# Down products of the scan stage summed over eight blocks instead of four, with two gate/up weight buffers

## The chip, the cores and the metric

The kernel runs on one core of one Trainium2 chip. The metric is the device time of one execution in microseconds, as the median of several runs. The engines are called PE (matrix products), DVE (vector), ACT (activation), POOL (GpSimd) and SP (which issues nearly all transfers of this stage, in one queue, in program order).

## The reference

Two layers work on x (4 x 512 tokens, 512 wide). Layer 0 is a cross attention and a feed-forward part; layer 1 a selective scan (an SSM whose input is the context and whose gate is x) and a mixture of 16 experts. The stage that matters here computes two parts at once: the feed-forward part of layer 0

```python
x = fwht(x * SU_ug) / SCALE
x_up = x @ W_up.T * (Wscale_ug[:INTER] * SCALE)
x_gate = x @ W_gate.T * (Wscale_ug[INTER:] * SCALE)
x = jax.nn.silu(x_gate) * x_up                        # 2048 wide
x = fwht(x * SU_dp) / SCALE
x = x @ W_down.T * (Wscale_dp * SCALE)                # back to 512
```

and the scan of layer 1, for 4 batches, 512 channels, 16 states, 512 steps

```python
state = state * exp(d_t * A) + (d_t * u_t) * B_t
y_t = einsum('ben,bn->be', state, C_t)
```

followed by `(y + D * u) * silu(z)`, which is added to x.

## The kernel before

`build` runs the stages one after another: norm, attention, prep, mix, norm and router, experts, combine. The change is in `stage_mix` (L1383), the scan stage. It has 64 blocks s, 16 (j) for each of 4 batches (b). A block does the work of one 128-wide slice of the 2048 hidden values and one state n of the scan, for 4 groups t of 128 channels. Each engine has its own program in a fixed order; semaphores are the only tie between them.

- PE, block s (L1623): `gate(s + 2)` and `up(s + 2)`, 12 products each of 512 columns; then `down(s - LAG)`, L1579: CHUNK = 4 fp32 products of 512 columns, which the profile shows as 8 passes, for one of the four groups of 128 tokens. So the downs of 4 blocks lie in the 4 blocks behind them, one token group in each, and each sums over CHUNK blocks in the one bank `ps_y`. Between them lie `turn` (j = 4, 5: transposes of the normed x), `rotate` (j = 7, 8, 10, 11: the Hadamard product of the next batch, 8 fp32 passes) and `turn_gated` (j = 12, 13). `up` has one bank, `ps_u`, and waits for the inner product before it.
- DVE, block s (L1914): `scan(4(s+1))`, `inner(s + 1)` (L1864: silu(gate) x up into `hT`), `add_y` (L1870: the down of the PE block before, from `ps_y` into the residual `xs`), `scan` twice, then what the block has besides (statistics at j = 0 to 3, `spread` at j = 4, low parts of the rotation at j = 8, 9, 11, 12, `add_gated` at 13, 14), and the last `scan`. A scan is the recurrence L1839 and the product with C, L1850; a group t = 0 also has an add, L1856.
- POOL (L1810): the driving products L1786 and the sums over states L1771, 7 operations in a block; at j = 1, 2, 3 `skip_add` (D x u, L1797 and L1799), at 8 to 11 `gated`. ACT: the decays and silu. Both state tiles (2) and drive tiles (4) are rings.
- SP (L1521), block s: `load_gu(s + 3)` (1 MB, waits for up of block s), `load_rows(s + 3)` (2 x 256 KB, waits for the products of block s - 1), at s % 4 == 3 `load_wd` (1 MB), then `load_u` at j = 0, 2, 3, `load_du` at j = 7 to 10 and `load_delta` at j = 11, 12, 14.
- Buffers: `gu` 3 x 1 MB, `wd` 2 x 1 MB, `hT` 2 x 4 slices, `delta` 6, `du` 8.

Of the kernel before, what the change touches and what calls it, by code (L numbers as in the profile page):

```python
# [17 lines left out]
P = 128  # L18
B = 4
S = 512  # L20
# [1362 lines left out]
def stage_mix(nc, xs, uT0, hs, guT, wdT, Wscale_ug, SU_dp, A_log, skip, u_d, delta_d, du_d, bc_d, ident):  # L1383
# [3 lines left out]
    ALL = B * BLOCKS  # L1387
    CHUNK = 4
    UNITS = BLOCKS * ET
    GU, ROWS, RING, BANKS = 3, 3, 4, 2  # L1390
    DELTAS, DUS = 6, 8
    LAG = CHUNK - 1
# [13 lines left out]
    with Scope(nc, "mix") as m:  # L1406
# [17 lines left out]
        gu = [m.sb(f"gu{i}", [P, 2, 2, KD, P], F32R) for i in range(GU)]  # L1424
        wd = [m.sb(f"wd{i}", [P, CHUNK, DIM]) for i in range(2)]
        sil = [m.sb(f"sil{i}", [P, S]) for i in range(2)]
        hT = [m.sb(f"hT{i}", [P, CHUNK, S]) for i in range(2)]
        delta = [m.sb(f"delta{i}", [P, S]) for i in range(DELTAS)]
# [13 lines left out]
        s_gu = [m.sem(f"gu_in{i}") for i in range(GU)]  # L1442
        s_wd = [m.sem(f"wd_in{i}") for i in range(2)]
        s_rows = [m.sem(f"rows_in{i}") for i in range(ROWS)]
# [13 lines left out]
        with m.block() as block:  # L1458
            @block.sync
            def _(sp):  # L1460
# [5 lines left out]
                def load_wd(n):  # L1466
                    if n >= 2:
                        sp.wait_ge(s_y, TB * (n - 1))
                    sp.dma_start(wd[n % 2][:, :, :], wdT[:, n % CHUNK * CHUNK:(n % CHUNK + 1) * CHUNK, :]).then_inc(s_wd[n % 2], 16)

# [44 lines left out]
                load_rows(1)  # L1515
                load_gu(2)
                load_rows(2)
                load_wd(0)
                load_wd(1)

                for s in range(ALL):  # L1521
                    b, j = divmod(s, BLOCKS)
                    if 3 <= s + 3 < ALL:
                        load_gu(s + 3)
                    if s + 3 < ALL:
                        load_rows(s + 3)
                    if s % CHUNK == CHUNK - 1 and 2 <= (s + 1) // CHUNK < ALL // CHUNK:
                        load_wd((s + 1) // CHUNK)
                    if b >= 1 and j == 0:
                        load_u(b - 1, 0)  # L1530
                        load_u(b - 1, 1)
                    if b >= 1 and j == 2:
                        load_u(b - 1, 2)
                    if b >= 1 and j == 3:
                        load_u(b - 1, 3)
                    if b + 1 < B and 7 <= j < 11:
                        load_du(ET * (b + 1) + j - 7)
                    if b + 1 < B and j in (11, 12):
                        load_delta(ET * (b + 1) + j - 11)
                    if b + 1 < B and j == BLOCKS - 2:  # L1540
                        load_delta(ET * (b + 1) + 2)
                        load_delta(ET * (b + 1) + 3)
# [4 lines left out]
            def _(pe):  # L1547
# [22 lines left out]
                def down(n):  # L1570
                    c, t = divmod(n, TB)
                    if t == 0:
                        pe.wait_ge(s_h, CHUNK * (c + 1))
                        pe.wait_ge(s_wd[c % 2], 16 * (c // 2 + 1))
                    if n:
                        pe.wait_ge(s_yadd, n)
                    tok = slice(t * P, (t + 1) * P)
                    for k in range(CHUNK):
                        mm = pe.matmul(ps_y[:, :], hT[c % 2][:, k, tok], wd[c % 2][:, k, :], start=(k == 0), stop=(k == CHUNK - 1))  # L1579
                    mm.then_inc(s_y, 1)  # L1580
# [42 lines left out]
                for s in range(ALL):  # L1623
                    b, j = divmod(s, BLOCKS)
                    if s + 2 < ALL:
                        gate(s + 2)
                        up(s + 2)
                    if s >= LAG:
                        down(s - LAG)
                    if b + 1 < B:  # L1630
# [14 lines left out]
                    if b >= 1:  # L1645
# [3 lines left out]
                        if j == 13:  # L1649
                            turn_gated(b - 1, 2)  # L1650
                            turn_gated(b - 1, 3)
                for n in range(ALL - LAG, ALL):
                    down(n)
# [176 lines left out]
            def _(dve):  # L1830
# [27 lines left out]
                def inner(n):  # L1858
                    j = n % BLOCKS
                    dve.wait_ge(s_up, n + 1)  # L1860
                    dve.wait_ge(s_silu, n + 1)
                    if n >= 2 * CHUNK and n % CHUNK == 0:
                        dve.wait_ge(s_y, TB * (n // CHUNK - 1))
                    dve.scalar_tensor_tensor(hT[n // CHUNK % 2][:, n % CHUNK, :], ps_u[:, :], upsc[:, j:j + 1],  # L1864
                                             sil[n % 2][:, :], ALU.mult, ALU.mult).then_inc(s_h, 1)

                def add_y(n):
                    dve.wait_ge(s_y, n + 1)
                    row = xs[:, n // BLOCKS * TB + n % TB, :]
                    dve.tensor_tensor(row, ps_y[:, :], row, ALU.add).then_inc(s_yadd, 1)  # L1870
# [4 lines left out]
                def gate_stats(b, t):  # L1875
                    dve.wait_ge(s_yadd, BLOCKS * b + (CHUNK - 1) * TB + t + 1)
                    own.mark(dve.bn_stats(stats[:, TB + t, :], xs[:, b * TB + t, :]))
# [36 lines left out]
                for s in range(ALL):  # L1914
                    b, j = divmod(s, BLOCKS)
                    q = ET * (s + 1)
                    if s + 1 < ALL:
                        scan(q)
                        inner(s + 1)
                    if s > LAG:  # L1920
                        add_y(s - LAG - 1)
                    if s + 1 < ALL:
# [29 lines left out]
                    if s + 1 < ALL:  # L1952
                        scan(q + 3)
                for n in range(ALL - LAG - 1, ALL):
                    add_y(n)
# [816 lines left out]
```

## Time and profile before

| | |
|---|---|
| median of 3 runs | 2685.6 us (2676.52 to 2686.33) |
| profiled execution | 2678.03 us, of which the span is 2676.2 us |
| mean granted clock of PE | 0.926 of full speed |
| scan stage | 1434 to 2175 us of the span |
| busy in the stage: PE, DVE, POOL, ACT | 660.2, 666.9, 606.5, 418.4 us of 741 |
| PE clock, transfers in the stage | 0.95; 171 GB/s |

The profile is one execution. A line of the timeline gives start, duration, engine, source line, the operation, what it writes and reads; a bracket at the end says how long the engine was idle before it and who ended that. A line of L1579 with x8 is eight passes, merged. Busy time isn't pace: the distance between two starts of the same operation (L1864 here, once in a block) is.

### The profile page before, as it was taken

The numbers are of one execution on the slowest core, as the hardware profiler recorded it, in microseconds if no ns is written. First come the engines' busy times: TensorE is split into PE (matmuls) and PEld (weight loads), VectorE is DVE, ScalarE is ACT, GpSimd is POOL, SyncE is SP. The second block draws the span as 40 slices with busy tenths as digits, with TensorE's granted clock in tenths as the row PEclk, the third lists the DMA queues.
The fourth block names the chain that finished last, engine by engine and source line by source line (L and its number), as shares of the span: only waits on it lengthen the run. The fifth ranks groups of instructions, "written<-read, shape, count | busy, mean of one in ns | idle before, by whom it ended". The sixth has DMA issues, their size and how long they took to land. (4 is left out here: it accounts for less than half of the span.)

```text
span 2676.2 us, 35075 instructions
## 1 busy us (share of the span) xinstructions
PE 2285.0 (85%) x10784; PEld 1760.5 (66%) x10785; DVE 1848.7 (69%) x3381; ACT 1229.4 (46%) x2129; POOL 1354.8 (51%) x1088
## 2 busy tenths in 40 slices
PE   3799999999999999998774998897998969468980
PEld 2688888878888888887433665665665547347770
DVE  6577776767676777766775999999999976312223
ACT  2344444544454544444573655655655622124430
POOL 0233333333333333333584888878978931678324
PEclk7799999999999999999887999998998988789995
DMA  7512232222323122220557555564665321765317
GB/s 283 221 67 88 87 111 88 85 74 84 111 87 112 68 87 87 87 88 20 185 194 226 173 183 189 172 197 142 208 183 163 122 83 48 248 170 176 121 51 263
DMA packets 136761, 363.49 MB, mean 136 GB/s; under 512 B 21264, under 2 KB 58768, under 8 KB 118416
## 3 DMA queue, kind: packets, MB, share of 16 engines
q1 hardware_dynamic: 123504, 328.30, 35.8%
q0 software_dynamic: 6320, 20.71, 2.5%
q10 hardware_dynamic: 6768, 12.32, 1.2%
q8 instruction: 94, 1.54, 0.2%
q14 instruction: 75, 0.61, 0.1%
HBM read 289.99 MB, written 71.30 MB: 135 GB/s over the span
## 5 line engine op out<-in xcount | busy, mean ns | idle before, releaser
L641 POOL TENSOR_SCALAR att_probs<-att_probs,att_recip 128x512 f32<-128x512 f32 x256 | 182.1, 714 | 560.8 <-DVE att_recip L708 560.8
L1786 POOL TENSOR_TENSOR mix_drive<-mix_du,mix_rows 128x512 f32<-128x512 f32 x256 | 326.7, 1283 | 63.0 <-DMA mix_rows<-bc_d 24.5
L565 ACT ACTIVATE att_probs<-att_s,att_bias,att_rq 128x512 f32<-128x512 f32 x256 | 200.5, 783 | 287.6 <-DVE att_bias L704 287.2
L1839 DVE TENSOR_TENSOR_SCAN mix_state<-mix_state,mix_drive 128x512 f32<-128x512 f32 x256 | 312.7, 1221 | 16.1 <-POOL mix_drive L1786 11.6
L1670 ACT ACTIVATE mix_state<-mix_delta,mix_a 128x512 f32<-128x512 f32 x256 | 176.7, 691 | 278.4 <-DVE mix_drive L1850 238.6
L1771 POOL TENSOR_TENSOR mix_y<-mix_y,mix_drive 128x512 f32<-128x512 f32 x180 | 230.8, 1282 | 78.7 <-DVE mix_drive L1850 78.7
L1579 PE MATMUL mix_down<-mix_wd,mix_hT 128*128 128x512 f32 x512 | 232.7, 597 | 8.6 <-DVE residual_x L1870 8.6
L703 DVE TENSOR_REDUCE att_nmax<-att_s 128x1 f32<-128x512 f32 x256 | 174.9, 683 | 69.3 <-PE att_s L101 62.0
L744 DVE TENSOR_TENSOR att_pT<-att_pt,att_pT 128x512 fp32r<-128x512 f32 x256 | 170.0, 685 | 65.6 <-ACT att_pT L571 61.6
L571 ACT CAST att_pT<-att_pt 128x512 fp32r<-128x512 f32 x256 | 144.2, 593 | 133.0 <-PE att_pt L422 128.7
L99 PE MATMUL att_w<-att_w_qkv,att_cx 128*128 128x256 f32 x512 | 158.4, 309 | 34.5 <-DVE att_w_qkv L690 26.4
L1579 PEld LDWEIGHTS mix_down<-mix_wd,mix_hT 128*128 128x128 f32 x512 | 97.5, 191 | 110.5 <-issue 96.2
L101 PE MATMUL att_w<-att_w_qkv,att_cx 128*128 128x256 f32 x512 | 152.5, 298 | 0.0
L100 PE MATMUL att_w<-att_w_qkv,att_cx 128*128 128x256 f32 x512 | 152.3, 297 | 0.0
L422 PE MATMUL att_pt<-att_ident,att_probs 128*128 128x128 f32 x1024 | 142.1, 277 | 6.6 <-DVE att_pT L744 2.3
L650 POOL TENSOR_TENSOR att_rq<-att_qss,att_power 128x8 f32<-128x8 f32 x32 | 55.6, 1737 | 159.2 <-DVE att_qss L740 159.2
L422 PEld LDWEIGHTS att_pt<-att_ident,att_probs 128*128 128x128 f32 x1024 | 118.8, 144 | 22.1 <-DVE att_pT L744 12.0
L99 PEld LDWEIGHTS att_w<-att_w_qkv,att_cx 128*128 128x128 f32 x512 | 105.0, 205 | 39.8 <-issue 37.3
L1850 DVE TENSOR_TENSOR mix_drive<-mix_state,mix_rows 128x512 f32<-128x512 f32 x180 | 124.4, 691 | 6.2
L99 PE MATMUL exp_g<-exp_w,exp_xT 128*128 x188 | 81.9, 436 | 53.2 <-POOL exp_w L2525 34.8
L579 ACT CAST att_oT<-att_o 128x512 fp32r<-128x512 f32 x64 | 37.7, 589 | 181.0 <-PE att_o L101 181.0
L99 PE MATMUL att_s<-att_kT,att_qT 128*128 128x512 f32 x256 | 106.7, 417 | 14.0 <-issue 9.1
(356 smaller groups left out, 6655.5 us busy)
## 6 DMA issues: line engine op xcount, KB each, us to landing
att_xn<-normT SPq DMA_DIRECT2D x32, 2048.0 KB, 8.7
mix_gu<-guT SPq DMA_DIRECT2D x64, 1024.0 KB, 8.2
mix_rows<-bc_d SPq DMA_DIRECT2D x128, 256.0 KB, 5.1
guT<-att_ffnT SPq DMA_DIRECT2D x32, 512.0 KB, 5.7
mix_wd<-wdT SPq DMA_DIRECT2D x16, 1024.0 KB, 7.8
slots<-exp_y ACTq DMA_DIRECT2D x47, 256.0 KB, 2.0
normT<-nrm_outT SPq DMA_DIRECT2D x4, 2048.0 KB, 9.1
exp_raw<-in_L_ffn_Wg SPq DMA_DIRECT2D x16, 512.0 KB, 5.8
```

The costliest lines, as they stand in the source:

```text
L99: pe.matmul(out, lh, rh, start=start, stop=False)
L101: return pe.matmul(out, ll, rh, start=False, stop=stop)
L422: tr = pe.transpose(ps_pt[(b + n) % 2][:, t, :], probs[:, h * TB + t, k * P:(k + 1) * P], ident_sb[:, :])
L565: act.activation(probs[:, n, :], ps_s[n % 2][:, :], ACT.Exp, bias=bias[:, n:n + 1], scale=rq[:, n:n + 1], accum_out=sums[:, n:n + 1]).then ...
L641: pool.tensor_scalar(probs[:, n, :], probs[:, n, :], recip[:, n:n + 1], 1.0, ALU.mult, ALU.mult).then_inc(s_pn, 1)
L703: own.after(dve.tensor_reduce(nmax[:, n:n + 1], ps_s[n % 2][:, :], AX_X, ALU.max, negate=True))
L744: dve.tensor_tensor(pT[:, 1, k, :], ps_pt[(b + (TB + 1) * h + k) % 2][:, :, :].rearrange("p t n -> p (t n)"), pT[:, 0, k, :].bitcast(F32), ...
L1579: mm = pe.matmul(ps_y[:, :], hT[c % 2][:, k, tok], wd[c % 2][:, k, :], start=(k == 0), stop=(k == CHUNK - 1))
L1670: act.activation(state[q % BANKS][:, :], delta[i % DELTAS][:, :], ACT.Exp, scale=a[:, t, n:n + 1]).then_inc(s_decay, 1)
L1771: pool.tensor_tensor(out[:, :], out[:, :], drive[q % RING][:, :], ALU.add).then_inc(s_padd, 1)
L1786: pool.tensor_tensor(drive[q % RING][:, :], du[i % DUS][:, :], rows[g % ROWS][:, 0, :], ALU.mult).then_inc(s_drive, 1)
L1839: dve.tensor_tensor_scan(h[:, :], h[:, :], drive[q % RING][:, :], 0.0, ALU.mult, ALU.add).then_inc(s_scan, 1)
```

## The change

Each down now sums over CHUNK = 8 blocks, so there are DOWNS = 32 of them instead of 64, each with 8 products (16 passes). They still take one token group at a time, one in each PE block, in the four blocks s with s - 7 = 0 to 3 modulo 8; the other four blocks have none. The adds follow, one block later. LAG grows from 3 to 7. `hT` becomes a ring of 14 single slices in place of two halves of 4. `wd` holds 8 slices (2 MB) in one buffer, and its load waits until all four downs of the chunk before are made; it is issued at s % 8 == 3 behind `load_rows`. `gu` has two buffers instead of three, and is loaded two blocks ahead; `du` has six instead of eight, and the last two tiles of a batch are loaded at j = 14.

```diff
@@ -1385,10 +1385,12 @@
     INTER = SU_dp.shape[0]
     BLOCKS = INTER // P
     ALL = B * BLOCKS
-    CHUNK = 4
+    CHUNK, INNERS = 8, 14
+    PER = TB * BLOCKS // CHUNK
+    DOWNS = B * PER
     UNITS = BLOCKS * ET
-    GU, ROWS, RING, BANKS = 3, 3, 4, 2
-    DELTAS, DUS = 6, 8
+    GU, ROWS, RING, BANKS = 2, 3, 4, 2
+    DELTAS, DUS = 6, 6
     LAG = CHUNK - 1
     SC = DIM ** -0.5
     assert BLOCKS == STATES
@@ -1422,9 +1424,9 @@
         normT = m.sb("normT", [P, KD, S])
         uT = [uT0, m.sb("uT1", [P, 2, KD, S], F32R)]
         gu = [m.sb(f"gu{i}", [P, 2, 2, KD, P], F32R) for i in range(GU)]
-        wd = [m.sb(f"wd{i}", [P, CHUNK, DIM]) for i in range(2)]
+        wd = m.sb("wd", [P, CHUNK, DIM])
         sil = [m.sb(f"sil{i}", [P, S]) for i in range(2)]
-        hT = [m.sb(f"hT{i}", [P, CHUNK, S]) for i in range(2)]
+        hT = [m.sb(f"hT{i}", [P, S]) for i in range(INNERS)]
         delta = [m.sb(f"delta{i}", [P, S]) for i in range(DELTAS)]
         du = [m.sb(f"du{i}", [P, S]) for i in range(DUS)]
         rows = [m.sb(f"rows{i}", [P, 2, S]) for i in range(ROWS)]
@@ -1440,7 +1442,7 @@
         s_a, s_aexp, s_neg = m.sem("a_in"), m.sem("a_exp_done"), m.sem("a_done")
         s_upsc = m.sem("up_scale_done")
         s_gu = [m.sem(f"gu_in{i}") for i in range(GU)]
-        s_wd = [m.sem(f"wd_in{i}") for i in range(2)]
+        s_wd = m.sem("wd_in")
         s_rows = [m.sem(f"rows_in{i}") for i in range(ROWS)]
         s_delta = [m.sem(f"delta_in{i}") for i in range(DELTAS)]
         s_du = [m.sem(f"du_in{i}") for i in range(DUS)]
@@ -1464,9 +1466,10 @@
                     sp.dma_start(gu[n % GU][:, :, :, :, :].bitcast(F32), guT[n % BLOCKS]).then_inc(s_gu[n % GU], 16)
 
                 def load_wd(n):
-                    if n >= 2:
-                        sp.wait_ge(s_y, TB * (n - 1))
-                    sp.dma_start(wd[n % 2][:, :, :], wdT[:, n % CHUNK * CHUNK:(n % CHUNK + 1) * CHUNK, :]).then_inc(s_wd[n % 2], 16)
+                    if n:
+                        sp.wait_ge(s_y, TB * n)
+                    at = n * CHUNK % BLOCKS
+                    sp.dma_start(wd[:, :, :], wdT[:, at:at + CHUNK, :]).then_inc(s_wd, 16)
 
                 def load_rows(g):
                     b, n = divmod(g, STATES)
@@ -1513,19 +1516,17 @@
                 sp.dma_start(d[:, :], skip.rearrange("(t p) -> p t", p=P), allow_slow_non_contiguous=True).then_inc(s_const, 16)
                 load_gu(1)
                 load_rows(1)
-                load_gu(2)
                 load_rows(2)
                 load_wd(0)
-                load_wd(1)
 
                 for s in range(ALL):
                     b, j = divmod(s, BLOCKS)
-                    if 3 <= s + 3 < ALL:
-                        load_gu(s + 3)
+                    if s + 2 < ALL:
+                        load_gu(s + 2)
                     if s + 3 < ALL:
                         load_rows(s + 3)
-                    if s % CHUNK == CHUNK - 1 and 2 <= (s + 1) // CHUNK < ALL // CHUNK:
-                        load_wd((s + 1) // CHUNK)
+                    if s > CHUNK and s % CHUNK == TB - 1:
+                        load_wd(s // CHUNK)
                     if b >= 1 and j == 0:
                         load_u(b - 1, 0)
                         load_u(b - 1, 1)
@@ -1533,11 +1534,13 @@
                         load_u(b - 1, 2)
                     if b >= 1 and j == 3:
                         load_u(b - 1, 3)
-                    if b + 1 < B and 7 <= j < 11:
+                    if b + 1 < B and j in (7, 8):
                         load_du(ET * (b + 1) + j - 7)
                     if b + 1 < B and j in (11, 12):
                         load_delta(ET * (b + 1) + j - 11)
                     if b + 1 < B and j == BLOCKS - 2:
+                        load_du(ET * (b + 1) + 2)
+                        load_du(ET * (b + 1) + 3)
                         load_delta(ET * (b + 1) + 2)
                         load_delta(ET * (b + 1) + 3)
                 for t in range(ET):
@@ -1571,12 +1574,12 @@
                     c, t = divmod(n, TB)
                     if t == 0:
                         pe.wait_ge(s_h, CHUNK * (c + 1))
-                        pe.wait_ge(s_wd[c % 2], 16 * (c // 2 + 1))
+                        pe.wait_ge(s_wd, 16 * (c + 1))
                     if n:
                         pe.wait_ge(s_yadd, n)
                     tok = slice(t * P, (t + 1) * P)
                     for k in range(CHUNK):
-                        mm = pe.matmul(ps_y[:, :], hT[c % 2][:, k, tok], wd[c % 2][:, k, :], start=(k == 0), stop=(k == CHUNK - 1))
+                        mm = pe.matmul(ps_y[:, :], hT[(c * CHUNK + k) % INNERS][:, tok], wd[:, k, :], start=(k == 0), stop=(k == CHUNK - 1))
                     mm.then_inc(s_y, 1)
 
                 def turn(b, t):
@@ -1625,8 +1628,9 @@
                     if s + 2 < ALL:
                         gate(s + 2)
                         up(s + 2)
-                    if s >= LAG:
-                        down(s - LAG)
+                    c, r = divmod(s - LAG, CHUNK)
+                    if s >= LAG and r < TB:
+                        down(c * TB + r)
                     if b + 1 < B:
                         if j == 4:
                             turn(b + 1, 0)
@@ -1649,7 +1653,7 @@
                         if j == 13:
                             turn_gated(b - 1, 2)
                             turn_gated(b - 1, 3)
-                for n in range(ALL - LAG, ALL):
+                for n in range(DOWNS - TB + 1, DOWNS):
                     down(n)
                 for t in range(TB):
                     turn_gated(B - 1, t)
@@ -1859,21 +1863,21 @@
                     j = n % BLOCKS
                     dve.wait_ge(s_up, n + 1)
                     dve.wait_ge(s_silu, n + 1)
-                    if n >= 2 * CHUNK and n % CHUNK == 0:
-                        dve.wait_ge(s_y, TB * (n // CHUNK - 1))
-                    dve.scalar_tensor_tensor(hT[n // CHUNK % 2][:, n % CHUNK, :], ps_u[:, :], upsc[:, j:j + 1],
+                    if n >= INNERS:
+                        dve.wait_ge(s_y, TB * ((n - INNERS) // CHUNK + 1))
+                    dve.scalar_tensor_tensor(hT[n % INNERS][:, :], ps_u[:, :], upsc[:, j:j + 1],
                                              sil[n % 2][:, :], ALU.mult, ALU.mult).then_inc(s_h, 1)
 
                 def add_y(n):
                     dve.wait_ge(s_y, n + 1)
-                    row = xs[:, n // BLOCKS * TB + n % TB, :]
+                    row = xs[:, n // PER * TB + n % TB, :]
                     dve.tensor_tensor(row, ps_y[:, :], row, ALU.add).then_inc(s_yadd, 1)
 
                 def normal_stats(b, t):
                     own.mark(dve.bn_stats(stats[:, t, :], xs[:, b * TB + t, :]))
 
                 def gate_stats(b, t):
-                    dve.wait_ge(s_yadd, BLOCKS * b + (CHUNK - 1) * TB + t + 1)
+                    dve.wait_ge(s_yadd, PER * (b + 1) - TB + t + 1)
                     own.mark(dve.bn_stats(stats[:, TB + t, :], xs[:, b * TB + t, :]))
 
                 def spread(first, last):
@@ -1917,8 +1921,9 @@
                     if s + 1 < ALL:
                         scan(q)
                         inner(s + 1)
-                    if s > LAG:
-                        add_y(s - LAG - 1)
+                    c, r = divmod(s - LAG - 1, CHUNK)
+                    if s > LAG and r < TB:
+                        add_y(c * TB + r)
                     if s + 1 < ALL:
                         scan(q + 1)
                         scan(q + 2)
@@ -1951,7 +1956,7 @@
                             add_gated(b - 1, 3)
                     if s + 1 < ALL:
                         scan(q + 3)
-                for n in range(ALL - LAG - 1, ALL):
+                for n in range(DOWNS - TB, DOWNS):
                     add_y(n)
                     gate_stats(B - 1, n % TB)
                 dve.wait_ge(s_z, TB * (B - 1))
```

## Rows read from the trace of the kernel before

**Rows 1.** The page, busy time, share of the span and instructions of each engine

```profile
PE 2285.0 (85%) x10784; PEld 1760.5 (66%) x10785; DVE 1848.7 (69%) x3381; ACT 1229.4 (46%) x2129; POOL 1354.8 (51%) x1088
```

**Rows 2.** Groups of the scan stage: count, busy us, mean ns, idle before, releasers

```profile
L1839 DVE TENSOR_TENSOR_SCAN mix_state<-mix_state,mix_drive 128x512 f32<-128x512 f32 x256 | 312.7, 1221 | 16.1 <-POOL mix_drive L1786 11.6 <-ACT mix_state L1670 4.5
L1579 PE MATMUL mix_down<-mix_wd,mix_hT 128*128 128x512 f32 x512 | 232.7, 597 | 8.6 <-DVE residual_x L1870 8.6
L1771 POOL TENSOR_TENSOR mix_y<-mix_y,mix_drive 128x512 f32<-128x512 f32 x180 | 230.8, 1282 | 78.7 <-DVE mix_drive L1850 78.7
```

**Rows 3.** Timeline of DVE, a plain block: start, us, operation, idle before

```profile
1523.96 0.75 DVE L1864 SCALAR_TENSOR_TENSOR mix_hT<-mix_up,mix_up_scale,mix_sil 128x512 f32<-128x512 f32 x1 [0.15 <-ACT mix_sil L1678]
1524.63 0.68 DVE L1870 TENSOR_TENSOR residual_x<-mix_down,residual_x 128x512 f32<-128x512 f32 x1
1525.23 1.22 DVE L1839 TENSOR_TENSOR_SCAN mix_state<-mix_state,mix_drive 128x512 f32<-128x512 f32 x1
...
1533.73 0.75 DVE L1864 SCALAR_TENSOR_TENSOR mix_hT<-mix_up,mix_up_scale,mix_sil 128x512 f32<-128x512 f32 x1 [0.16 <-ACT mix_sil L1678]
```

**Rows 4.** Timeline of PE, a block with a down and a rotation

```profile
1524.77 0.51 PE L99 MATMUL mix_up<-first_uT,mix_gu 128*128 128x512 f32 x1
...
1527.65 3.59 PE L1579 MATMUL mix_down<-mix_wd,mix_hT 128*128 128x512 f32 x8
1531.09 3.60 PE L1601 MATMUL mix_spare<-mix_normT,first_hs 128*128 128x512 f32 x8
1534.12 0.79 PE L99 MATMUL mix_gate<-first_uT,mix_gu 128*128 128x512 f32 x1
...
1537.28 0.39 PE L99 MATMUL mix_up<-first_uT,mix_gu 128*128 128x512 f32 x1
```

**Rows 5.** Adds of DVE that wait for a down: one of them, and all

```profile
1589.72 0.69 DVE L1870 TENSOR_TENSOR residual_x<-mix_down,residual_x 128x512 f32<-128x512 f32 x1 [1.91 <-PE mix_down L1579]
...
  DVE residual_x L1870: 24.9, 13
```

**Rows 6.** PE after blocks without a down, and the clock of that stretch

```profile
1479.71 0.51 PE L99 MATMUL mix_up<-first_uT,mix_gu 128*128 128x512 f32 x1 [2.36 <-DVE mix_hT L1864]
...
1484.16 2.31 PE L1579 MATMUL mix_down<-mix_wd,mix_hT 128*128 128x512 f32 x5
...
1450.00:1484.00 34.00, 25.25 (x88) 19.32 (x87) 32.72 (x40) 20.83 (x25) 28.89 (x23) 0.85 0.57 176
```

**Rows 7.** SP, POOL and DVE around u, block j = 3, batch 1

```profile
1649.79 0.43 SPq L1500 DMA_DIRECT2D mix_work<-u_d  x1
...
1658.76 1.56 POOL L1797 TENSOR_SCALAR mix_work<-mix_work,mix_skip 128x512 f32<-128x512 f32 x1 [1.43 <-DMA mix_work<-u_d]
...
1663.03 1.23 DVE L1839 TENSOR_TENSOR_SCAN mix_state<-mix_state,mix_drive 128x512 f32<-128x512 f32 x1 [2.58 <-POOL mix_drive L1786]
```

**Rows 8.** Transfers: the page's median landing; 1648 to 1661 us in 40 slices

```profile
mix_gu<-guT SPq DMA_DIRECT2D x64, 1024.0 KB, 8.2
...
GB/s 0 0 0 0 63 195 176 164 95 82 113 88 50 101 158 258 315 303 340 347 328 384 391 391 435 447 378 410 454 429 479 391 378 328 202 101 50 25 25 0
...
mix_gu<-guT SPq DMA_DIRECT2D x1, 1024.0 KB, 10.8
```

**Rows 9.** SP and DVE: a load of gu is issued, L1864 follows

```profile
1691.57 0.43 SPq L1464 DMA_DIRECT2D mix_gu<-guT  x1
...
1693.53 0.75 DVE L1864 SCALAR_TENSOR_TENSOR mix_hT<-mix_up,mix_up_scale,mix_sil 128x512 f32<-128x512 f32 x1
```

**Rows 10.** DVE, the last inner product and the last adds

```profile
2134.28 0.75 DVE L1864 SCALAR_TENSOR_TENSOR mix_hT<-mix_up,mix_up_scale,mix_sil 128x512 f32<-128x512 f32 x1 [0.16 <-ACT mix_sil L1678]
...
2146.86 0.69 DVE L1870 TENSOR_TENSOR residual_x<-mix_down,residual_x 128x512 f32<-128x512 f32 x1 [3.85 <-PE mix_down L1579]
...
2151.35 0.69 DVE L1870 TENSOR_TENSOR residual_x<-mix_down,residual_x 128x512 f32<-128x512 f32 x1 [3.06 <-PE mix_down L1579]
...
2160.31 0.69 DVE L1870 TENSOR_TENSOR residual_x<-mix_down,residual_x 128x512 f32<-128x512 f32 x1 [3.06 <-PE mix_down L1579]
```

## Prediction

> **What bounds the kernel now.** I read the page first, for busy shares over the whole span [rows 1], then the groups of the scan stage alone (1434 to 2175 us, 741 us long) [rows 2], then the order of time of single blocks on DVE and on PE [rows 3, 4], and last the lines with an idle time in brackets [rows 5 to 7]. No engine's share of the whole span says anything on a change to one stage; the spacing of blocks does. The reader is to see in [rows 3] that DVE's inner product L1864 comes again after 9.77 us (1523.96 to 1533.73), with only 0.16 us of idle time ahead of it: in a plain block DVE sets the pace. The add L1870 costs it 0.60 us there (1524.63 to the scan at 1525.23).
>
> PE is close behind. From [rows 4]: up starts 0.81 us after L1864 (whose 0.75 us it must await, for `ps_u` has one bank), the down follows up by 2.88 us, eight passes of it take 3.59 us (3.44 us until the next fp32 product can start), gate starts 3.03 us after the last group of eight began, and the next up 3.16 us after gate. A block costs PE 3.03 + 3.16 + about 2.8 = 8.9 us with a down, and 3.44 us more with a rotation, so 12.4 us. Where rotations lie, PE falls back and DVE's adds wait for the down [rows 5]: 1.91 us in that row, 24.9 us in 13 waits in all. Four of these are at the end of the stage (3.85 and three of 3.06 us, together 13.0) [rows 10], so nine inside are worth 11.9 us. That wait decides this change: in program order the add of a down stands right behind the inner product of the next block, so DVE gives a down hardly a block's time.
>
> **The change part by part.** I write b for the batch, j for the block in it, and "burst" for the four blocks in a row that now hold a long down.
>
> (1) Removed: 32 of 64 adds. One, at the stage's end, leaves a wait and not a block; 31 × 0.60 = -18.6 us. POOL is the next engine there: it has 7 products of 1.28 us in a block and only 0.65 to 0.7 us idle in a plain one (78.7 us over the stage [rows 2]), so it nearly fills 9.1 of the new 9.17 us. If it takes half the gain, the term is -9; I take -18.6, as POOL's waits are on DVE.
>
> (2) Moved: the same 512 passes on PE, but 16 in each of four blocks and none in the next four. A long down takes 15 × 0.43 + 0.59 = 7.03 us, from 3.44/8 = 0.43 us a pass [rows 4]. The first add of a burst is wanted 9.17 + 0.67 = 9.84 us after the last L1864; the down ends at 0.81 + 2.88 + 7.03 = 10.72: wait 0.9 us. After that PE's block is 8.9 + 3.44 = 12.35 us without and 15.8 us with a rotation, and each add of a burst waits for what DVE's block lacks of it. DVE's blocks: 9.77 us plain; an estimate from the add's 0.60 us for each further 128x512 operation (statistics, low part of a rotation).
> - Bursts in the middle of batches 0 to 2 (adds at j = 8 to 11; rotations in PE's blocks 7 and 8, so between adds 0, 1 and 2): 0.9 + (15.8 - 10.4) × 2 + (12.3 - 9.8) = 14.2 us each, 42.6 in all.
> - Bursts at the start of batches 1 and 2 (adds at j = 0 to 3, two statistics a block): 0.9 + 3 × (12.35 - 10.95) = 5.1 each; batch 3 (one statistic): 0.9 + 3 × 2.1 = 7.2; together 17.4.
> - The burst in the middle of batch 3, no rotation: 0.9 + 3 × 2.57 = 8.6.
> Sum +68.6 us. The nine waits of 11.9 us that are there now lie in blocks j = 11 to 15, which have no down afterwards: -11.9.
>
> (3) PE's clock. Blocks without a down exist today, at the stage's start: with gaps of 2.4 to 3.9 us the mean granted clock of that stretch is 0.85 and up-to-down takes 1484.16 - 1479.71 = 4.45 us instead of 2.88 [rows 6]: the engine came out of its gap at the lower of its two levels (1.2 GHz). Before each of the seven bursts there are now such blocks (PE has 5.6 us of work in 9.17). Bounds 0 and 1.57 us a burst; I take half, 0.8 × 7 = +5.6, since the late weights (5) will split the gap.
> The Trainium skill speaks against the change here ("TensorE: Matmul & The Clock Gate", the section on why this matters): keep the engine fed, as gaps between bursts of products return it to half its clock. The trace agrees, by [rows 6]. By that rule in full the term is +11.0.
>
> (4) `wd` has one buffer of 2 MB instead of two of 1 MB. Its load waits on SP for the burst's last down (L1467, `s_y`), and what is queued behind it there are, at j = 3, `load_u(b - 1, 3)`, and the next weights. Today u is issued at 1649.79 behind an already free `wd`, and POOL starts with it at 1658.76 after waiting 1.43 us; the chain through POOL reaches DVE's scan at 1663.03, 4.27 us later, which waited 2.58 [rows 7]. Afterwards u is issued when the last down of the burst has ended. It then took 8.9 us to land, with half a megabyte of rows and 1 MB of wd ahead; now 2 MB ahead, at the near 400 GB/s of [rows 8] 2.6 us more, and the rows gone before: 8 us (bounds 7.5 and 11.5). The scan can start 0.8 + 8 + 4.27 = 13.0 us after the down's end. DVE would want it after an add, three scans and the statistics, at 7.5 (batch 3: 6.9): +5.5, +5.5, +6.1 = +17.1. All seven waits of scans for POOL now there, 11.6 us [rows 2], are in blocks 3 to 5 of batches 1 to 3, and the burst's delays give POOL the time: -11.6. The load itself has four blocks (37 us) before the next burst needs it.
> The Trainium skill ("Trainium Kernel Development and Optimization", Best Practices) says to double-buffer so that transfers lie beside compute; by that the single `wd` would stall PE. The trace speaks against a stall of PE, with 8 us of landing against 37, and for one of what is queued behind.
>
> (5) `gu` with two buffers. Each load has the same wait as before (up of block s), and is issued as now, 1.96 us ahead of L1864 [rows 9], but is used one block earlier. It lands 8.2 us after issue, behind a wd after 10.8 [rows 8]: 6.2 us after L1864, where gate could have started at 3.6. Gate then ends at 9.1, before up may start (9.97). Cost 0 to DVE; if the load comes 5 us later in a burst's first block, up to 5 us a burst.
> (6) `du` with six buffers: tiles 2 and 3 are loaded at j = 14, with delta 2 and 3 as now; half a megabyte more, 1.3 us, with their use a block later: 0. `hT` as ring of 14: inner(14) awaits a down that ended two blocks before: 0.
> (7) The stage's end. Today the last add starts 2160.31 - 2134.28 = 26.0 us after the last L1864, in steps of 4.49 us [rows 10]. Afterwards the first long down takes about 8.8 us from a cold engine and starts at 0.9, the other three come in steps of 4.49 + 3.44 = 7.93: 0.9 + 8.8 + 3 × 7.93 = 33.5: +7.5.
>
> Sum: -18.6 + 68.6 - 11.9 + 5.6 + 17.1 - 11.6 + 7.5 = +56.7 us, on the profiled execution's 2678.0: 2734.7. That execution is 7.6 us under the median of three, between the lowest and the others; half of that gives 2738. Bounds: without clock and u terms +45; with the whole clock term, u at its late end and half the saving +80.
>
> **The rivals.**
> - *Faster: PE absorbs the bursts.* The adds are what counts, DVE goes on as the bound, PE runs ahead in the light blocks: -18.6, 2659. It decides at the first add of a burst: the long down must end within 9.84 us of the last L1864, which needs passes of 0.37 us or PE more than a block ahead. Against it: up waits for L1864 in each block, so no lead is kept over light blocks, and [rows 5]. Within it lies "no change", where half is absorbed by slack that I have not seen.
> - *Half of it.* PE's lead at a burst's start is larger than I allow, or u lands in time, or blocks with statistics hide the rest: +25 to +35, about 2708. For it: blocks 4 to 6 are long, and DVE has slack in none but these.
> - *The loads decide.* 2 MB in front of gu at j = 3 and 11, gate misses its weights by 5 us in each of seven bursts: +35 on top, 2770. For it: 10.8 us of landing in [rows 8], above the median; against it: in my sum gate wants them 11 us after their issue.
> - *It doesn't do what it says*: the ring or the one `wd` makes DVE wait in every block. By the counts in (6) it does not.
>
> **How the numbers follow.** My case (+45 to +80, 2723 to 2758) 0.65, half of it 0.13, loads 0.12, no change 0.05, faster 0.05. Within 0.5% (13 us) is what a measurement here can't tell from no change. The range leaves out the two last and some of the loads: 2702 to 2768. Faster 0.05, same 0.05, slower 0.90.
>
> **What would show it.** Right: DVE waits on `mix_down` of some 70 us over four blocks in eight, with 5.4 us at the adds behind rotations; L1870 32 times; the spacing of L1864 at 9.17 us in light blocks, 12.3 in bursts, 15.8 behind rotations; the scan of j = 4 waiting 5 us for POOL, and POOL for u; up from a cold clock at the first block of a burst. Wrong: adds without a wait in a burst (the first rival), or PE's gate waiting for `mix_gu` (the third).

## The result, and the profile after

The changed kernel takes 2749.25 us (median of 4 runs, 2745.28 to 2750.74) against 2681.06 us of the kernel before (4 runs): a ratio of 1.0252, 95% interval 1.0229 to 1.0275. Run again beside another experiment it gave 1.0246 (1.0226 to 1.0265). So it is some 66 to 69 us slower; 57 us had been forecast, and the time lies inside the stated range.

The scan stage, taken from the first inner product to the last add of a down, lasts 779.3 us in the profiled execution instead of 716.1: +63.1. The stages ahead of it, whose code is the same, took 6.3 us longer in that execution. Over the twelve profiled executions of this study, whose kernels are alike up to there but for the stage's own first loads, the first inner product starts anywhere from 1444.2 to 1452.3 us. So I compare stage lengths below wherever a few microseconds count. A stage length is that of one execution; the two of the changed kernel are 2.4 us apart (779.3 and 781.7).

The page, busy time after (the row that answers to [rows 1]), and the groups of the stage that answer to [rows 2]:

```profile
PE 2301.7 (84%) x10784; PEld 1771.6 (65%) x10785; DVE 1835.3 (67%) x3349; ACT 1228.6 (45%) x2129; POOL 1354.3 (49%) x1088
...
L1843 DVE TENSOR_TENSOR_SCAN mix_state<-mix_state,mix_drive 128x512 f32<-128x512 f32 x256 | 312.6, 1221 | 24.3 <-POOL mix_drive L1790 19.0 <-ACT mix_state L1674 5.1
L1775 POOL TENSOR_TENSOR mix_y<-mix_y,mix_drive 128x512 f32<-128x512 f32 x180 | 230.4, 1280 | 113.5 <-DVE mix_drive L1854 112.9
L1582 PE MATMUL mix_down<-mix_wd,mix_hT 128*128 128x512 f32 x512 | 226.8, 596 | 6.3 <-DVE mix_hT L1868 4.0 <-DVE residual_x L1874 2.4
```

DVE has 32 instructions fewer and less work, and yet the kernel is slower. PE still does 512 passes at the same price. What grew is idle time. Here is all of the adds' waiting, from the view of the `mix_down` tile (who waited for it: us, times), in place of the 24.9 us of [rows 5]:

```profile
  DVE residual_x L1874: 94.7, 32
```

A light block and a block of a burst on DVE (timeline; answers to [rows 3]):

```profile
1519.31 0.75 DVE L1868 SCALAR_TENSOR_TENSOR mix_hT<-mix_up,mix_up_scale,mix_sil 128x512 f32<-128x512 f32 x1
1519.98 1.22 DVE L1843 TENSOR_TENSOR_SCAN mix_state<-mix_state,mix_drive 128x512 f32<-128x512 f32 x1
...
1528.49 0.75 DVE L1868 SCALAR_TENSOR_TENSOR mix_hT<-mix_up,mix_up_scale,mix_sil 128x512 f32<-128x512 f32 x1 [0.17 <-ACT mix_sil L1682]
...
1548.92 0.75 DVE L1868 SCALAR_TENSOR_TENSOR mix_hT<-mix_up,mix_up_scale,mix_sil 128x512 f32<-128x512 f32 x1 [0.16 <-ACT mix_sil L1682]
1555.02 0.69 DVE L1874 TENSOR_TENSOR residual_x<-mix_down,residual_x 128x512 f32<-128x512 f32 x1 [5.35 <-PE mix_down L1582]
...
1564.74 0.75 DVE L1868 SCALAR_TENSOR_TENSOR mix_hT<-mix_up,mix_up_scale,mix_sil 128x512 f32<-128x512 f32 x1 [0.17 <-ACT mix_sil L1682]
```

Without its add a block takes 9.18 us, for the 9.17 of the sum; inside a burst, behind a rotation, 15.82 us, of which the add waits 5.35. PE in that burst (answers to [rows 4]):

```profile
1529.29 0.50 PE L99 MATMUL mix_up<-first_uT,mix_gu 128*128 128x512 f32 x1 [1.01 <-DVE mix_hT L1868]
...
1532.15 7.03 PE L1582 MATMUL mix_down<-mix_wd,mix_hT 128*128 128x512 f32 x16
1539.02 3.60 PE L1604 MATMUL mix_spare<-mix_normT,first_hs 128*128 128x512 f32 x8
1542.05 0.79 PE L99 MATMUL mix_gate<-first_uT,mix_gu 128*128 128x512 f32 x1
...
1545.21 0.39 PE L99 MATMUL mix_up<-first_uT,mix_gu 128*128 128x512 f32 x1
```

From up to up PE needs 15.92 us here, with no idle time between; a plain block of a burst is 12.32 us in DVE's spacing. The down is 7.03 us long, and starts 2.86 us after up: PE came into this burst at its full clock.

### The profile page after: what moved, and what is told of

Its sections match the earlier page's. It is cut to its first block and busy times, and to the rows that moved or that the text cites. A ratio compares the mean times of both kernels' runs of the same rounds, so it can differ in the third digit from the quotient of the medians.

```text
span 2743.5 us, 35027 instructions
## 1 busy us (share of the span) xinstructions
PE 2301.7 (84%) x10784; PEld 1771.6 (65%) x10785; DVE 1835.3 (67%) x3349; ACT 1228.6 (45%) x2129; POOL 1354.3 (49%) x1088
## 3 DMA queue, kind: packets, MB, share of 16 engines
q10 hardware_dynamic: 6768, 12.32, 1.2%
## 5 line engine op out<-in xcount | busy, mean ns | idle before, releaser
L1582 PE MATMUL mix_down<-mix_wd,mix_hT 128*128 128x512 f32 x512 | 226.8, 596 | 6.3 <-DVE mix_hT L1868 4.0
L99 PE MATMUL att_w<-att_w_qkv,att_cx 128*128 128x256 f32 x512 | 158.0, 309 | 34.4 <-DVE att_w_qkv L690 26.2
```

The lines of the kernel that those rows point to most:

```text
L99: pe.matmul(out, lh, rh, start=start, stop=False)
L1582: mm = pe.matmul(ps_y[:, :], hT[(c * CHUNK + k) % INNERS][:, tok], wd[:, k, :], start=(k == 0), stop=(k == CHUNK - 1))
```

## The experiments

Ten runs in three groups, beside the two kernels; each run's ratio is to the kernel before on its own chip.

| run | ratio to before (95%) | stage, us | adds' waits before the stage's end | scans for POOL |
|---|---|---|---|---|
| before | 1 | 716.1 | 11.8 | 11.6 |
| after | 1.0252 (1.0229 to 1.0275) | 779.3 | 73.3 | 19.0 |
| after again | 1.0246 (1.0226 to 1.0265) | 781.7 | 75.4 | 19.0 |
| two gu buffers alone | 0.9991 (0.9977 to 1.0005) | 714.4 | 11.2 | 10.3 |
| and six du | 0.9988 (0.9975 to 1.0001) | 715.4 | 12.1 | 10.7 |
| half the products | 0.9920 (0.9901 to 0.9939) | 695.9 | 7.1 | 17.4 |
| u first | 1.0153 (1.0136 to 1.0170) | 760.6 | 75.4 | 0 |
| add late | 1.0239 (1.0213 to 1.0265) | 781.0 | 33.7 | 29.8 |
| gu ahead of du | 1.0229 (1.0205 to 1.0254) | 774.6 | 68.3 | 19.0 |
| three orders | 1.0111 (1.0087 to 1.0134) | 744.8 | 29.2 | 0 |
| spread | 1.0050 (1.0030 to 1.0069) | 726.9 | 12.5 | 0 |
| short rotation | 1.0181 (1.0164 to 1.0198) | 765.2 | 59.5 | 18.8 |

The two last columns are sums of the bracketed idle times of the add and of the scan over the stage's timeline.

### Do the buffers cost anything? (e1, e1b)

```diff
-    GU, ROWS, RING, BANKS = 3, 3, 4, 2
+    GU, ROWS, RING, BANKS = 2, 3, 4, 2
...
-                load_gu(2)
...
-                    if 3 <= s + 3 < ALL:
-                        load_gu(s + 3)
+                    if s + 2 < ALL:
+                        load_gu(s + 2)
```

> The kernel before with two gate/up buffers instead of three (loads two blocks ahead), and nothing else. Theory (long downs on PE are the cost, the buffers are nearly free): gate wants its weights about 6.7 us after L1864 and they land 6.2 us after it, so 0 to +6 us against before, most of it behind loads of wd. Rival (the loads decide): gate stalls on weights in many blocks and DVE with it, +15 us or more.

> The run before it, and six du buffers with tiles 2 and 3 loaded at j = 14 as in the changed kernel. Theory: the half megabyte more ahead of gate's weights makes gate 2 to 3 us late once in a batch, 3 to 6 us in all on top of the run with two gate/up buffers. Rival (this is where the late start of the bursts at j = 15 comes from and it stands alone): 10 us or more on top.

Measured: 0.9991 and 0.9988, stages of 714.4 and 715.4 us. Two buffers cost nothing that the times or the stages show, and neither does the later load of du; the 3 to 6 us that I had expected for that one on top did not appear. Gate does wait for its weights, in e1:

```profile
PEld mix_gate L99 <- DMA mix_gu<-guT: 27.3, 17, 3.1
```

These 27.3 us fall on an engine that would otherwise have waited for the inner product: its waits for that fell from 56.5 to 40.6 us. The price paid for the memory was nothing here; the loss lies in what the memory bought.

### Is it the length of the downs? (e2)

```diff
-                    for k in range(CHUNK):
-                        mm = pe.matmul(..., start=(k == 0), stop=(k == CHUNK - 1))
+                    for k in range(4):
+                        mm = pe.matmul(..., start=(k == 0), stop=(k == 3))
```

> The changed kernel with only 4 of the 8 products in each down (slices 4 to 7 of each chunk are left out of the sum), so that a down has its old length while the adds stay halved and all loads stay as changed. Theory (burst length): waits of the add L1874 for the down fall from 94.7 us to below 15 (the stage's end), and the time is before - 18.6 (adds) - 11.9 (old waits) + 8 (u behind 2 MB of wd) = before - 22 us. Rival (loads, or the DVE itself): still 30 us or more above before.

Measured: 0.9920, which is 21.5 us less than before (2661.37 against 2684.11 as medians, 22.7). All adds together wait 16.3 us, a little over the 15 that I had expected. It is the change nearly without its cost: what halving the adds would be worth if PE could deliver a sum over eight as quickly as one over four. Of the stage's 20.2 us, though, 5.0 lie behind the last inner product (21.1 us to the last add instead of 26.0), where passes are simply missing; my expectation had no term for them. So 15.3 us are the gain in the blocks. PE's work is halved with the downs, so this run alone doesn't tell bursts from too much work on PE; the kernel before does, for it has the same 512 passes in a stage of 716.1 us. The loads are as in the changed kernel, so the loads alone are ruled out as its cause. The scans still wait 17.4 us for POOL: 2 MB of wd stand in front of u even where the last down ends early, and POOL waits 3.86 us for u at j = 3 of batch 1.

### The wait that hangs on wd (e3)

```diff
-                    if s > CHUNK and s % CHUNK == TB - 1:
-                        load_wd(s // CHUNK)
...
                     if b >= 1 and j == 3:
                         load_u(b - 1, 3)
+                    if s > CHUNK and s % CHUNK == TB - 1:
+                        load_wd(s // CHUNK)
```

> The changed kernel with the load of u at j = 3 issued ahead of the load of wd, which waits for the burst's last down. Theory: POOL no longer waits 6.85 us for u, the three waits of scans for POOL (5.84, 6.37, 6.78 us) go, 15 to 19 us less than the changed kernel, about +50 us against before instead of +68. Rival (the wait only moves, to gate's weights behind the 2 MB): no more than 5 us less.

After, around j = 3 of batch 1: SP issues wd as soon as the last down has ended, then u; POOL starts with u 8.7 us later, and the scan of the next block waits (answers to [rows 7]):

```profile
1670.83 0.32 SPq L1472 DMA_DIRECT2D mix_wd<-wdT  x1
1671.19 0.43 SPq L1503 DMA_DIRECT2D mix_work<-u_d  x1
...
1679.90 1.56 POOL L1801 TENSOR_SCALAR mix_work<-mix_work,mix_skip 128x512 f32<-128x512 f32 x1 [6.85 <-DMA mix_work<-u_d]
...
1684.14 1.23 DVE L1843 TENSOR_TENSOR_SCAN mix_state<-mix_state,mix_drive 128x512 f32<-128x512 f32 x1 [5.84 <-POOL mix_drive L1790]
```

With u first:

```profile
1666.21 0.43 SPq L1503 DMA_DIRECT2D mix_work<-u_d  x1
1670.19 0.32 SPq L1472 DMA_DIRECT2D mix_wd<-wdT  x1
...
1672.38 1.57 POOL L1801 TENSOR_SCALAR mix_work<-mix_work,mix_skip 128x512 f32<-128x512 f32 x1
```

POOL starts without waiting, no scan waits for POOL any more, and the stage is 18.7 us shorter. The difference of the ratios (1.0252 - 1.0153, some 27 us) is larger than that, but with the two intervals it is anything from 19 to 34 us. The chain is shown: last down, SP's wait, u, POOL, scan.

### Where the add stands (e4)

```diff
-                    c, r = divmod(s - LAG - 1, CHUNK)
-                    if s > LAG and r < TB:
-                        add_y(c * TB + r)
                     if s + 1 < ALL:
                         scan(q + 1)
                         scan(q + 2)
+                    c, r = divmod(s - LAG - 1, CHUNK)
+                    if s > LAG and r < TB:
+                        add_y(c * TB + r)
```

> The changed kernel with DVE's add of a down moved behind the next two scans of its block (3.7 us later in DVE's order). Theory (a long down is late only against where the add stands, and PE's blocks of 12.3 and 15.8 us set the rest): each of the seven bursts loses 3.7 us of its waits once, at its first adds, and keeps the others; 20 to 26 us less than the changed kernel, so +42 to +48 us against before. Rival (PE alone sets the pace of a burst from its first block): within 5 us of the changed kernel.

Measured: 1.0239, a stage of 781.0 us: nothing gained. My theory missed, and the rival's number (within 5 us) came out. The adds' waits did fall, from 73.3 to 33.7 us, as each stands 3.7 us later. But the time went into other waits:

```profile
1556.53 0.69 DVE L1874 TENSOR_TENSOR residual_x<-mix_down,residual_x 128x512 f32<-128x512 f32 x1 [1.88 <-PE mix_down L1582]
1560.60 0.69 DVE L1896 SCALAR_TENSOR_TENSOR mix_uT<-mix_spare,mix_uT 128x512 fp32r<-128x512 f32 x1 [3.37 <-ACT mix_uT L1705]
...
1685.55 1.23 DVE L1843 TENSOR_TENSOR_SCAN mix_state<-mix_state,mix_drive 128x512 f32<-128x512 f32 x1 [9.68 <-POOL mix_drive L1790]
```

Behind a long down PE makes the rotation, so DVE waits 3.37 us for that instead (by way of ACT, which reads PE's product first); 1.88 + 3.37 is about the 5.35 that the add waited in the changed kernel. And u is issued at the end of the last down, which PE sets: the scan that waited 5.84 us waits 9.68. DVE ran ahead and came to the same places at the same time.

### The start of a burst (e6)

```diff
-                    if s + 2 < ALL:
+                    if s + 2 < ALL and not (j == BLOCKS - 1 and b + 1 < B):
                         load_gu(s + 2)
...
                     if b + 1 < B and j == BLOCKS - 2:
+                        load_gu(s + 3)
                         load_du(ET * (b + 1) + 2)
```

> The changed kernel with gate's weights for the first block of a burst at a batch's start issued ahead of the four du and delta tiles of j = 14 instead of behind them. Theory: gate no longer waits 3.1 us for weights there and comes out of a shorter gap; the first waits of these three bursts (2.56, 3.73, 3.65 us) fall to about 1: 5 to 8 us less than the changed kernel. Rival (PE's lower clock after light blocks makes that lateness): no more than 2 us less.

After, at the start of batch 1: weights issued at 1611.84, behind four tiles of du and delta, and gate waits for them, then runs slowly (up comes 4.45 us after gate's start, instead of 3.16 behind a down in [rows 4]):

```profile
1610.82 0.97 SPq L1488 DMA_DIRECT2D mix_delta<-delta_d  x2
1611.84 0.43 SPq L1466 DMA_DIRECT2D mix_gu<-guT  x1
...
1619.61 0.50 PE L99 MATMUL mix_gate<-mix_uT,mix_gu 128*128 128x512 f32 x1 [3.11 <-DMA mix_gu<-guT]
1624.06 0.40 PE L99 MATMUL mix_up<-mix_uT,mix_gu 128*128 128x512 f32 x1
...
1633.87 0.69 DVE L1874 TENSOR_TENSOR residual_x<-mix_down,residual_x 128x512 f32<-128x512 f32 x1 [2.56 <-PE mix_down L1582]
```

With the weights ahead:

```profile
1617.77 0.50 PE L99 MATMUL mix_gate<-mix_uT,mix_gu 128*128 128x512 f32 x1 [2.23 <-DMA mix_gu<-guT]
...
1632.05 0.69 DVE L1875 TENSOR_TENSOR residual_x<-mix_down,residual_x 128x512 f32<-128x512 f32 x1 [0.83 <-PE mix_down L1583]
```

The first waits of the three bursts fell from 2.56, 3.73 and 3.65 us (3.68, 4.00 and 3.58 in the second execution of the changed kernel) to 0.83, 0.83 and 2.41, and the stage by 4.7 us. As a time, 1.0229 against 1.0252 and 1.0246 can't be told apart; the trace shows the step, the times don't resolve it.

What is left of the third above 0.83 us is the rival's part, PE's lower clock. In front of that burst gate waited 2.13 us and up another 2.23, and the down starts 4.44 us after up instead of 2.87; the mean granted clock from 2013 to 2018 us is 0.66:

```profile
2008.02 0.50 PE L99 MATMUL mix_gate<-mix_uT,mix_gu 128*128 128x512 f32 x1 [2.13 <-DMA mix_gu<-guT]
...
2013.27 0.50 PE L99 MATMUL mix_up<-mix_uT,mix_gu 128*128 128x512 f32 x1 [2.23 <-DVE mix_hT L1869]
...
2017.71 7.03 PE L1583 MATMUL mix_down<-mix_wd,mix_hT 128*128 128x512 f32 x16
```

### Taken together, and spread out (e7, e5)

e7 holds the edits of e3, e4 and e6. e5 adds to it, for the middle of each batch:

```diff
+    MIDDLE = {7: (0, 0, 1), 8: (0, 1, 2), 9: (1, 0, 2), 10: (2, 0, 1), 11: (2, 1, 2), 12: (3, 0, 1), 13: (3, 1, 2)}
+    MIDDLE_ADDS = {9: 0, 10: 1, 12: 2, 14: 3}
...
+                    if s >= LAG and j in MIDDLE:
+                        t, first, last = MIDDLE[j]
+                        down(2 * b * TB + t, first, last)
```

where first and last say which halves (8 passes each) of token group t are made in block j; wd is loaded in halves.

> The three changes of order together (u ahead of wd, the add behind two scans, gate's weights ahead of du and delta), with the long downs as they are. Theory: they are separate costs and add up, save for the third, which the later add hides: 68 - 27 - 24 - 2 = about +15 us against before, and what is left are the waits behind rotations. Rival: they overlap, +30 us or more.

> The run with the three orders, and the four long downs in the middle of each batch laid over seven blocks (j = 7 to 13) as three downs in two halves of 8 passes and one long one; wd is then loaded in two halves. The adds stay halved. Theory (even work on PE is what the old chunks gave): the waits behind rotations nearly go, 8 to 9 us for each of batches 0 to 2 and 4 us for batch 3, so 25 to 30 us less than the run before it: 10 to 15 us faster than the kernel before. Rival (halving the adds can't pay as other engines or PE's total work bound the stage): no faster than before.

e7 measured 1.0111, about +30 us; I had hoped for +15. Its stage is 34.4 us shorter than after's, though the three alone gave 18.7, 4.7 and -1.7. By the stages, then, the late add, worth nothing alone, is worth 8 to 13 us once u no longer hangs on the last down (13 against the first execution of the changed kernel, 8 against the second). The times don't resolve that: e7 is 11 us below e3, with e6's 6 us in it, and that difference is uncertain by some 8 us either way. The rival's number came out, the reason that it gave did not, by the stages: there the parts don't overlap. My +15 failed because it took 24 us for the late add, which e4 had not yet shown to gain nothing by itself.

e5 measured 1.0050 (1.0030 to 1.0069), 16 to 20 us less than e7 (by ratios and by medians) and still slower than before, where I expected a gain; the rival's number came out. Up to the last inner product it has caught up: 688.5 us against 690.1 of before. The rest is the stage's end, 38.4 us instead of 26.0:

```profile
2133.49 0.75 DVE L1882 SCALAR_TENSOR_TENSOR mix_hT<-mix_up,mix_up_scale,mix_sil 128x512 f32<-128x512 f32 x1
2137.88 0.68 DVE L1888 TENSOR_TENSOR residual_x<-mix_down,residual_x 128x512 f32<-128x512 f32 x1
...
2148.16 0.69 DVE L1888 TENSOR_TENSOR residual_x<-mix_down,residual_x 128x512 f32<-128x512 f32 x1 [6.53 <-PE mix_down L1593]
```

The first of the last four long downs had to wait for the add at 2137.88, which frees the bank and which I had put late; that is 5 us, for with all downs long and the add late too e7's end takes 33.3. Besides, the ring of 14 slices makes four inner products wait for a down, 10.2 us together:

```profile
1592.27 0.75 DVE L1882 SCALAR_TENSOR_TENSOR mix_hT<-mix_up,mix_up_scale,mix_sil 128x512 f32<-128x512 f32 x1 [3.18 <-PE mix_down L1593]
```

And 14.8 us are waits for rotations. So of the 30 blocks that are lighter by 0.6 us, hardly anything is left. The waits for the ring and at the end come from how this run was laid out, not from halving the adds, so it doesn't show that halving can't pay; no run does without them.

### The rotations' share (e9)

```diff
-                    for k in range(KD):
+                    for k in range(1):
                         g = 0 if hadamard_sign(k, o) > 0 else 1
-                        mm = pe.matmul(..., stop=(k == KD - 1))
+                        mm = pe.matmul(..., stop=(k == 0))
```

> The changed kernel with one product instead of four in each rotation (three quarters of the Hadamard sum are left out), so that a rotation takes 2 passes. Theory (long downs pile up on rotations): PE's block falls from 15.8 to about 13.2 us, the adds' waits of 5.3 us to about 2.8, the bursts in the middle of batches 0 to 2 from 14 to 9 us of waits: 15 us less than the changed kernel, +50 us against before. Rival (rotations don't matter, a long down alone does it): no more than 5 us less.

> The changed kernel once more, on the chip of the run with short rotations, as its measure: +63 to +72 us against before, with a stage of 779 us.

Measured: 1.0181 against 1.0246 on the same chip, 17 us less, and a stage shorter by 16.5. The adds behind rotations:

```profile
1549.07 0.69 DVE L1874 TENSOR_TENSOR residual_x<-mix_down,residual_x 128x512 f32<-128x512 f32 x1 [2.77 <-PE mix_down L1582]
...
1562.30 0.69 DVE L1874 TENSOR_TENSOR residual_x<-mix_down,residual_x 128x512 f32<-128x512 f32 x1 [2.76 <-PE mix_down L1582]
```

5.35 became 2.77, just by the 2.6 us that PE's block lost: in a burst the add's wait is PE's block less DVE's. Most of the bursts' waits need no full rotation: 59.5 of 75.4 us are left. Even a block of a burst without one takes 12.32 us.

## Why the prediction was right

By its own steps:

- **Adds saved (1), -18.6 us.** Most light blocks without other work are 9.15 to 9.18 us, as forecast. But the sum over the stage is only about -13: with the measured waits, 73.3 - 11.8 + 19.0 - 11.6 + 7.2 (the end) = 76.1, and the stage grew by 63.1. This is the term that was mis-sized, by 5.6 us, and the traces account for nearly all of it. First, only 30 adds leave the blocks (58 stand ahead of the last inner product before, 28 after), not 31. Second, the blocks from j = 5 to 6 of batches 1 to 3 are hardly shorter (18.05, 18.07 and 17.74 us against 18.05, 18.04 and 17.98), 1.6 us. In them DVE works through a chain of small operations, and in both kernels each that takes over a microsecond ends within 0.05 us of the end of a POOL product; once POOL is idle they all take 0.17 us or less. In batches 1 and 2 the add saved is lost again in L1889, 1.20 us instead of the 0.60 of L1885 before:

```profile
1690.56 2.49 POOL L1790 TENSOR_TENSOR mix_drive<-mix_du,mix_rows 128x512 f32<-128x512 f32 x2
1691.87 1.20 DVE L1889 TENSOR_SCALAR mix_var_eps<-mix_meanvar 128x8 f32<-128x8 f32 x1
1693.01 1.26 POOL L1775 TENSOR_TENSOR mix_y<-mix_y,mix_drive 128x512 f32<-128x512 f32 x1
1693.11 1.18 DVE L107 TENSOR_SCALAR mix_guess<-mix_var_eps 128x8 int32<-128x8 int32 x1
```

So POOL did take a part there, though by no wait that the profile names; why a small operation of DVE ends with POOL's, no run shows. It took no more than that, far from the half that I gave as a bound. Third, one up is late by 0.99 us. Fourth, an add that waits no longer runs into the inner product before it: the spacing of blocks in bursts exceeds the old one plus the wait by some 0.1 us each (15.82 - 5.35 = 10.47 against 10.37), about 2.5 us over 28 adds.
- **Bursts (2), +68.6 us.** The mechanism and the sizes held. Middle of batches 0 to 2: 0.81, 5.35, 5.34, 2.51 us in the first, 14.0, 13.8 and 13.9 in all, for 14.2. Middle of batch 3: 8.1 for 8.6. Start of batches: 6.4, 7.8 and 9.3 for 5.1, 5.1 and 7.2. The excess is in their first adds alone. All 28 adds inside the stage wait.
- **Clock (3), +5.6 us.** The size came out (7.2 us, the excess just named), but with luck, for the reason is only half right: I had spread it over seven bursts, and it lies in three. In front of the four middle bursts the gaps were split, as (5) had guessed: gate waits 2.1 us for weights, up 1.0 for DVE, and the mean granted clock from 1510 to 1530 us is 0.98; nothing was lost there. In front of the three others a gate waited 3.1, 5.4 and 5.7 us for weights and came out late and at the lower level, 1.2 GHz (its 12 products take 4.5, 5.0 and 4.6 us instead of 3.16 until up starts). e6 shows that the order of loads did most of it: with weights ahead of du and delta two of three waits are back at 0.83, and the third keeps 1.6 us of lower clock. Step (5) had the weights issued 1.96 us ahead of the inner product; in front of the burst of batch 1 they are issued level with it (1611.84 and 1611.82 us), behind four tiles. In (6) I had priced that load of du at nothing, and e1b bears this out for the old chunks; in front of a burst it was not free. I had read the rule of the Trainium skill on keeping the engine fed ("TensorE: Matmul & The Clock Gate", on why this matters) as worth 11.0 us in full, an estimate; the trace gave less, as the engine had fewer long gaps than bursts.
- **u behind wd (4), +17.1 us for 11.6.** Measured 19.0 for 11.6, with u's landing at 8.7 us for the 8 assumed. e3 shows the chain. The Trainium skill's advice to double-buffer ("Trainium Kernel Development and Optimization", Best Practices) was to the point in its result: with one buffer scans waited 19.0 us for POOL, with two 11.6. But no product waited for that buffer, as the trace had said; a tile queued behind the load did, and an exchange of two lines took it away.
- **Two gu buffers (5), 0.** e1: 0.9991. In the changed kernel the same loads were not free in front of three bursts, as said under (3).
- **The end (7), +7.5 us.** 33.18 us from the last inner product to the last add, where it was 26.03: +7.2. It comes in steps of 7.92 us, for the 7.93 of the sum (answers to [rows 10]):

```profile
2196.59 0.75 DVE L1868 SCALAR_TENSOR_TENSOR mix_hT<-mix_up,mix_up_scale,mix_sil 128x512 f32<-128x512 f32 x1
...
2206.02 0.69 DVE L1874 TENSOR_TENSOR residual_x<-mix_down,residual_x 128x512 f32<-128x512 f32 x1 [1.90 <-PE mix_down L1582]
...
2213.94 0.69 DVE L1874 TENSOR_TENSOR residual_x<-mix_down,residual_x 128x512 f32<-128x512 f32 x1 [6.50 <-PE mix_down L1582]
```

The sum for the stage was 56.7 and came to 63.1: 5.6 more by the term of the adds, 1.9 by u, and 0.9 less by bursts and clock together, 0.3 less by the end. The mechanism forecast is the one measured. Of the rivals, e2 prices the first: the gain would have been there, about 15 us in the blocks, had PE delivered in time. Half of it (+25 to +35) is out with 63 to 66. Of the third, the sign that I had named did appear, gate waiting for its weights in the changed kernel (waits: us, times, longest):

```profile
PE mix_gate L99 <- DMA mix_gu<-guT: 57.8, 17, 6.5
```

But it cost no 35 us: e1 and e2 run the same two buffers without loss, and here these waits show at no more than the first adds, 7.2 us, and the one late up. The fourth (DVE waits in every block) is out with the light blocks of 9.15 to 9.18 us.

What stays open: how POOL's products come to end DVE's small operations, and why the medians differ by 68 and 69 us where the stages differ by 63 and 66; the times at which the stage begins vary by more than that over the twelve executions.

## What to carry to other kernels

Summing over more before an add saves the add, and makes the producer's work come in bursts. Where the producer has only its own block's time to spare, the consumer pays the burst's excess in each block of it, and no light block gives it back, because the single `up` bank lets PE get no more than one product ahead (the trace shows up waiting for the inner product in light blocks, 1.01 us in the line above; a second bank was not tried). So compare block against block, not the sums over a stage: PE's sum is the same 512 passes as before, and yet 5.35 us too much in one block was paid in full. A wait moved later is not removed if other work of the same producer is queued behind it. And where a load must wait for something, put what does not depend on it ahead of it in the queue; that was the cheapest 19 us here.

## What was not expected of the hardware

A stage whose code is the same, fed by the same inputs, began at times 8 us apart (1444.2 to 1452.3 us) in twelve profiled executions, as much as several terms of the sum. Ten of these kernels differ in the stage itself; the two executions of the changed kernel began 1.9 us apart. Differences of a few microseconds were readable only within the stage.
